# A gap in the scratch of the query and key parts: loads in runs of 2 KB, stores per batch

## The reference

```python
# layer 0: one head over all 1024 features, causal; ffn: 8 experts (shared weights + LoRA), top 2
# layer 1: attention of 16 heads, each the difference of two softmaxes over halves of 8 features
Q, K, V = (proj(Wq), proj(Wk), proj(Wv))                  # (b, 16, n, 16)
Q1, Q2 = jnp.split(Q, 2, axis=-1); K1, K2 = jnp.split(K, 2, axis=-1)
A1 = where(causal, Q1 @ K1.T * scaling, -inf); A2 = where(causal, Q2 @ K2.T * scaling, -inf)
attn = softmax(A1) - lam * softmax(A2)
O = attn @ V; O = O / rms(O) * rms_scale * (1 - LAMBDA_INIT); s = O @ Wo.T
# layer 1 ffn: 32 experts of 64 inner features (gate, up, down), top 8 by sigmoid, and a shared one
```

## Time and profile before

| | |
|---|---|
| median of 3 runs | 596.47 us (593.23 to 597.14) |
| the profiled execution, own time | 595.78 us |
| its span in the trace | 593.8 us |
| PE busy | 495.8 us (83%) |
| DVE, ACT, POOL busy | 393.3, 288.0, 266.4 us |
| mean granted TensorE clock | 0.934 of full |
| moved by DMA | 46.02 MB in 30,842 packets |

### The profile page before, as it was taken

How to read it: one execution, slowest core, us unless ns; L and a number is a source line. 1 busy time by engine, 2 the same in 40 slices (tenths; PEclk the granted TensorE clock), 3 DMA queues, 4 the chain that set the end, 5 groups by cost and what they waited for, 6 DMA issues and landing times.

```text
span 593.8 us, 8610 instructions
## 1 busy us (share of the span) xinstructions
PE 495.8 (83%) x3104; PEld 238.9 (40%) x3104; DVE 393.3 (66%) x796; ACT 288.0 (48%) x460; POOL 266.4 (45%) x223
## 2 busy tenths in 40 slices
PE   4865883988996999989947998999984991999995
PEld 4532631443443454443514453444431450444442
DVE  2426612879986786689844894669892971785674
ACT  1432450056775344576642445447660571447742
POOL 6122230134766406446431367326653364327973
PEclk9996796999999899999986999899996996899999
DMA  8502442212241311113330132013430142112111
GB/s 295 199 1 63 118 123 81 81 57 55 74 124 57 98 71 54 54 54 107 100 104 19 36 85 86 11 54 90 137 104 31 41 104 71 43 35 75 37 35 37
DMA packets 30842, 46.02 MB, mean 78 GB/s; under 512 B 4464, under 2 KB 18896, under 8 KB 28624
## 3 DMA queue, kind: packets, MB, share of 16 engines
q1 hardware_dynamic: 30800, 45.47, 25.4%
HBM read 37.47 MB, written 7.60 MB: 76 GB/s over the span
## 4 chain that ended last, share of the span: by engine, by line
PE 42%; DMA 24%; DVE 12%; SPq 10%; ACT 4%; issue 4%; POOL 3%; POOLq 1%; DVEq 0%; ACTq 0%
DMA ka<-parts_scratch 23%; SPq L515 8%; PE bank L728 6%; PE bank L737 5%; PE bank L749 5%; PE scores L769 4%; PE scores L763 4%; DVE nmax L1271 3%; PE scores L679 2%; PE bank L824 2%; PE scores L702 2%; PE bank L850 1%; DVE tmp L1124 1%; POOL gb L1070 1%; PE bank L837 1%
## 5 line engine op out<-in xcount | busy, mean ns | idle before, releaser
L1271 DVE TENSOR_REDUCE nmax<-scores 128x4 f32<-128x1024 f32 (+1 forms) x96 | 113.9, 1218 | 82.7 <-PE scores L769 82.3
L1070 POOL TENSOR_TENSOR gb<-gb,wb 128x512 f32<-128x512 f32 x64 | 84.1, 1314 | 155.6 <-ACT gb L978 145.2
L1063 POOL TENSOR_SCALAR_AFFINE_SELECT pk<-pk 128x512 f32<-128x512 f32 (+1 forms) x96 | 82.9, 872 | 80.4 <-ACT pk L991 79.7
L991 ACT ACTIVATE pk<-scores 128x1024 f32<-128x1024 f32 x96 | 95.6, 1024 | 40.2 <-PE scores L769 40.0
L975 ACT ACTIVATE gt<-bank,bgh 128x512 f32<-128x512 f32 (+1 forms) x68 | 46.8, 688 | 90.4 <-PE bank L728 81.5
L763 PE MATMUL scores<-mask_h,ident_h 64*128 64x256 bf16 (+2 forms) x384 | 40.1, 288 | 57.2 <-DMA ka<-parts_scratch 53.8
L728 PE MATMUL bank<-xnt,wg 128*128 128x512 f32 x128 | 72.1, 646 | 0.0
L749 PE MATMUL bank<-h,wd 128*128 128x512 f32 x128 | 69.6, 638 | 0.0
L737 PE MATMUL bank<-xnt,wu 128*128 128x512 f32 x128 | 68.5, 617 | 0.8 <-DVE h L1250 0.7
L1243 DVE SCALAR_TENSOR_TENSOR h<-gt,gb 128x512 f32<-128x512 f32 x64 | 50.3, 786 | 17.3 <-POOL gb L1070 12.5
L1250 DVE SCALAR_TENSOR_TENSOR h<-bank,bu,h 128x512 f32<-128x512 f32 x64 | 48.1, 751 | 16.4 <-PE bank L737 14.5
(11 more groups left out here) (191 smaller groups left out, 738.3 us busy)
## 6 DMA issues: line engine op xcount, KB each, us to landing
wb<-wt_scratch SPq DMA_DIRECT2D x64, 256.0 KB, 4.1
parts_scratch<-parts SPq DMA_DIRECT2D x48, 128.0 KB, 2.0
qa<-parts_scratch SPq DMA_DIRECT2D x16, 192.0 KB
ka<-parts_scratch SPq DMA_DIRECT2D x16, 192.0 KB
qa<-parts_scratch SPq DMA_DIRECT2D x16, 128.0 KB
ka<-parts_scratch SPq DMA_DIRECT2D x16, 128.0 KB
x<-in_x SPq DMA_DIRECT2D x4, 256.0 KB, 2.6
ha<-in_wkq SPq DMA_DIRECT2D x1, 1024.0 KB, 4.9
```

The costliest lines, as they stand in the source:

```text
L991: A(dst.rearrange("p (h m) q -> p m h q", m=2), pairs[pair_of(step)][:, :, :].rearrange("p m (h q) -> p m h q", q=cols), ACT.Exp, scale=SC ...
L1063: pool.affine_select(out=dst, in_=dst, compare_op=ALU.is_ge, fill=0.0, base=0, pattern=[[0, heads], [1, P]], channel_multiplier=-1).then_i ...
L1070: pw(gb[:, c % 2, :], gb[:, c % 2, :], wb[:, k % 2, j % 2, :], ALU.mult).then_inc(s_ga_done, 1)
L1271: V.tensor_reduce(dst, src, AX, ALU.max, negate=True).then_inc(s_nmax_done, 1)
```

## The change

The scratch gets a gap behind every fourth head: its last two dimensions (16 heads, 256 tokens) become (4 groups, 4 + 1 heads, 256 tokens), of which the fifth head is never written or read. A row of 16 heads is then four runs of 1,024 elements (2 KB), 2.5 KB apart. The loads of `fetch` name four runs for each row; their number (12 in a fetch), their rows and their bytes stay. The stores no longer fit one access pattern for both batches, so each is issued once for each batch: 24 of 64 KB in a chunk in place of 12 of 128 KB, still in runs of 512 bytes. The waits count the larger number of stores.

```diff
-                   qk_ps=4, qk_rest=4, part1=4, part2=4, part3=4, parts_stored=16 * 12, v_ps=2, v_sb=2,
+                   qk_ps=4, qk_rest=4, part1=4, part2=4, part3=4, parts_stored=16 * 24, v_ps=2, v_sb=2,
...
                                     sp.wait_ge(done, at(c, name, 2 * n + f + 1))
-                                    dst = t["parts_dram"][c, n, :, r, f * DH:(f + 1) * DH, :, :]
-                                    sp.dma_start(dst.rearrange("b d h t -> (d h) b t"),
-                                                 parts[:, a, 2 * n + f, :].rearrange("p (b t) -> p b t", b=CB)).then_inc(s_parts_stored, 16)
+                                    for b in range(CB):
+                                        dst = t["parts_dram"][c, n, b, r, f * DH:(f + 1) * DH, :, 0:GH, :]
+                                        sp.dma_start(dst.rearrange("d g h t -> (d g) h t"),
+                                                     parts[:, a, 2 * n + f, b * SEQ:(b + 1) * SEQ]).then_inc(s_parts_stored, 16)
...
-                                    src = t["parts_dram"][c, n, b, first:first + width, m * DH:(m + 1) * DH, :, :]
+                                    src = t["parts_dram"][c, n, b, first:first + width, m * DH:(m + 1) * DH, :, 0:GH, :]
                                     sp.dma_start(dst[row:row + width * DH, b, :, :], src).then_inc(s_qk_in[b], 16)
...
-    t["parts_dram"] = nc.dram_tensor("parts_scratch", (CHUNKS, 2, CB, 3, 2 * DH, HEADS, SEQ), BF16, kind="Internal").ap()
+    t["parts_dram"] = nc.dram_tensor("parts_scratch", (CHUNKS, 2, CB, 3, 2 * DH, GROUPS, GH + 1, SEQ), BF16, kind="Internal").ap()
```

More of the change, by code:

```diff
@@ L498, in steps @@
                                     sp.wait_ge(done, at(c, name, 2 * n + f + 1))
-                                    dst = t["parts_dram"][c, n, :, r, f * DH:(f + 1) * DH, :, :]
-                                    sp.dma_start(dst.rearrange("b d h t -> (d h) b t"),
-                                                 parts[:, a, 2 * n + f, :].rearrange("p (b t) -> p b t", b=CB)).then_inc(s_parts_stored, 16)
+                                    for b in range(CB):
+                                        dst = t["parts_dram"][c, n, b, r, f * DH:(f + 1) * DH, :, 0:GH, :]
+                                        sp.dma_start(dst.rearrange("d g h t -> (d g) h t"),
+                                                     parts[:, a, 2 * n + f, b * SEQ:(b + 1) * SEQ]).then_inc(s_parts_stored, 16)
                     elif kind == "fetch":
                         b = rest[0]
-                        sp.wait_ge(s_parts_stored, at(c, "parts_stored", 16 * 12))
+                        sp.wait_ge(s_parts_stored, at(c, "parts_stored", 16 * 24))
                         if c:
@@ L932, in front @@
                     if c and name == "queries1":
-                        act.wait_ge(s_parts_stored, at(c - 1, "parts_stored", 16 * 12))
+                        act.wait_ge(s_parts_stored, at(c - 1, "parts_stored", 16 * 24))
                     first = 0 if name == "queries1" else 2
```

## The result

The changed kernel takes **623.67 us** (median of 4 runs, 623.05 to 625.26) against 596.81 for the kernel before: ratio 1.0468, interval 1.0422 to 1.0513. It is slower by 26.9 us; the forecast was 611.0 with a range of 599 to 622. The direction was right and the size too small, and the time lies outside the range. The profiled execution takes 625.26 us, its span is 623.2 us.

The account below looks back on a forecast made before the run. Bound by `ka` fetches that two of sixteen engines carry while PE waits. Loads 9.1 + PE's clock 0.9 + stores 4.7 and 0.5 = 15.2 us on the profiled 595.78 gives 611.0 us, range 599 to 622.

Parts of the forecast that it names:

- What bounds the kernel: Fetches of `ka`: seven on the chain, each bound by two engines holding 68 rows; PE idles 53.8 us for them.
- The loads: Four 2 KB packets in place of one 8 KB: 1.3 us more a fetch, +9.1 us over seven fetches.
- the `x` window: Load of `x` alone, 48.0 to 49.6 us: 2 KB in 87 ns, +13% a row, 2.65 us a fetch.
- The stores: 12 more for each chunk on SP at 0.46 us, 24 in 11.0 us: chunk 1 +4.7, chunk 3 +0.5.
- The cover: Gaps and following waits on SP hide the extra stores: chunks 0 and 2 cost nothing, chunk 3 +0.5 us.
- SP held in a fetch: If the queue counts packets, SP is held amid each fetch; costed at nothing, as later work uses the same engines.
- rival 3: SP stuck within fetches, `wb` loads behind four of them start late: +10, so 621 us; chance 0.25 together with rival 4.
- Rival 4: Load packets cost what the `x` row gives or more: 18.6 for 9.1, 620.5 us; chance 0.25 together with rival 3.
- PE's clock: Longer fetch 1/1 makes PE idle, so one pair of matmuls runs at the 1.2 GHz level: +0.9 us (0 to 2).
- Rival 2: The gap spreads the reads, so fetches end faster: 581 us, or 590 with 9.1 for packets; chance 0.11.

Follow-up runs that it names:

- The order by half: Kernel before with the scratch reordered so a load's rows follow with one pitch, no gap, 12 stores in a chunk: 537.74 us, ratio 0.900.
- with 12 stores: Changed kernel storing batch 0 alone, 12 stores of 64 KB in a chunk, both batches loading batch 0's parts: 606.69 us, ratio 1.0187.
- plain stores: Kernel before with 24 stores in a chunk, one for each batch, no gap, loads unchanged: 603.71 us, ratio 1.014.

## Why the prediction was wrong, point by point

1. **What bounds the kernel: right.** Fetches that two engines carry and PE waits for. With the same bytes spread over more engines, 50 of the 53.8 us of PE's waits went. The order by half was chosen by the Trainium skill's rule on the number of engines (DMA: Bandwidth & Descriptors, "Why a DMA increments its semaphore by 16 and not by 1"), and the trace agrees that more engines then work: the share reaches 1.00, and the count of small packets fits 36 engines for three loads in place of 13.
2. **The loads: right in kind, smaller than forecast.** Predicted +9.1 over seven fetches, measured +6.1, and +6.6 with 12 stores. The tail of a fetch in the changed kernel has PE idle and two engines at 51 GB/s where it was 53:

```profile
203.00:209.00 6.00, 0.00 (x0) 0.00 (x0) 0.00 (x0) 0.00 (x0) 0.00 (x0) 0.50 0.13 51
```

   That is 4% and not the 6% I took, let alone the 13% of the `x` window, much of which may be its start, as I had noted. Tails of other fetches differ by 2% only (51 and 50, 49 and 48 GB/s in windows of 5 us), so this rate is known to a few per cent; the sum of the fetches, +6.1 against 1.0 with unchanged loads, is the firmer number. The Trainium skill's 3 cycles a packet (DMA: Bandwidth & Descriptors, "Why small descriptors are slow (HBM only)") made it 5.1 us, nearer than my sum. For 512 bytes the same rule gives 16 x 19 cycles against 259, an estimate of 17% of 7 x 21.0, 25.5 us; 37.8 were measured, so it is too mild there, if nothing but the packets made these fetches longer.
3. **The stores: this is the step that failed.** "Half the bytes in each issue take that away, so I take 0.46" gave 24 stores 11.0 us. They take 15.5 to 15.8 in chunks 0, 2 and 3, 0.645 to 0.66 from issue to issue, and 16.7 in chunk 1. I had priced them from eight DMAs of 16 partitions and from the old stores, whose two sides have equal shapes; the row in the order of instructions, 32x4x256 against 128 partitions, was in front of me, and I read no price for an unequal shape off it, though the kernel before had one: loads with 24 rows against 3 x 8 cost SP 0.70 us, the plain ones of 8 rows 0.43. With plain stores at 0.43 the step comes out nearly as forecast, +7.1 against 5.2, though 24 of them still take 12.0 to 12.5 us and not 11.0.
4. **The cover: right for the assumed price, gone with the real one.** Chunks 0, 2 and 3 had 12.4, 11.8 and 11.4 us for the stores. 11.0 fit, 15.5 do not; each lost 3.6 to 4.2 us where I had 0, 0 and 0.5, and chunk 1 lost 10.2 for 4.7. In chunks 2 and 3 the sum had no term for the maxima's rows behind the stores, for which PE now waits 3.4 and 3.0 us. Of the 16.8 us that the sum lacks in the stores, 11.3 are here and 5.5 in chunk 1. I kept an upper end of 0.53 us for the price, which gives some 9 us of stores by the same covers and not 22.0. The range reached 622 only through rivals 3 and 4, whose causes did not come, so that it ends so near the measured time is luck.
5. **SP held in a fetch: seen, and nearly free,** as costed. SP needs 15.4 to 17.4 us for a fetch's issues and not 7.7, and what stands behind the fetches is not later for it: from the landing of fetch 0/0 to the next store 61.1 us pass against 62.2, behind 2/0 28.6 against 28.8, behind 3/1 87.7 against 89.0. Only behind 2/1 it is 42.4 against 40.9, with PE at a colder clock (next point). So rival 3, with its 621 us the nearest number, had the hold right and its price wrong. That the fetch itself is no longer for the hold is likely, since its sum grew by 6.1 us only, but no run has the packets without the hold. Rival 4 wanted 18.6 us for the packets; 6.1 rule it out.
6. **PE's clock: +0.9 did not come where I put it.** After fetch 1/1 the granted clock stayed at 1.00, the level of 2.4 GHz, though PE had waited 1.9 us for that fetch and not 0.6:

```profile
245.80:252.00 6.20, 6.04 (x38) 2.95 (x39) 5.25 (x6) 0.57 (x1) 5.80 (x2) 1.00 0.28 95
```

   A colder clock came after fetch 2/1 instead. The same three microseconds, from 3 us behind its landing, before and after:

```profile
374.57:377.57 3.00, 3.00 (x7) 1.31 (x6) 0.85 (x2) 1.15 (x2) 0.00 (x0) 0.76 0.00 1
```

```profile
399.09:402.09 3.00, 3.00 (x5) 1.35 (x4) 1.38 (x2) 0.12 (x1) 0.00 (x0) 0.50 0.01 3
```

   PE had waited 4.3 us for that fetch and not 3.3. The stretch from its landing to chunk 3's first store is 1.5 us longer (42.4 for 40.9, mean clock 0.92 for 0.96), inside the 0 to 2 that I had given for the clock, at another fetch; it lies in "all the rest" of the table.

7. **Rival 2, a gap that spreads the reads:** nothing of it. With gaps behind every eighth, fourth or each head no fetch on the chain was shorter by more than 0.8 us, and their sum grew each time, with the gap behind every eighth head by no more than unchanged loads do.

Sum by the runs: 22.0 (stores) + 6.1 (loads) = 28.1 against 15.2 forecast; the profiled executions differ by 29.5, of which 3.0 are start-up, and the medians by 26.9. PE's wait for `ka` came to 66.2 us, close to the 68 I had named, but that is luck: the loads gave less and chunk 1's stores more, where this wait went from 4.8 to 16.2 us.

## What to carry to other kernels

A DMA has a price on the queue that issues it, apart from its bytes, and it depends on how its two sides are cut: take it from a DMA of the same shape on both sides as yours, and multiply it by the count before calling it hidden, since a cover of 11.8 us hides 11.0 and not 15.5. When a transfer bounds a kernel, divide its rate by the rate of one engine first: here two of sixteen carried it, and reordering the scratch so that a load's rows have one pitch was worth 10%, while cutting its runs from 8 to 2 KB cost 1% (to 512 bytes, 7%). When a queue fills, time from last issue to landing shrinks without anything getting faster; measure from the first issue.

## What the runs showed of the hardware that was not expected

- SP's time for a DMA from the same queue: 0.29 to 0.35 us for loads of 8 to 24 rows, whole on both sides, one after the other, 0.43 for plain stores of 128 runs back to back, 0.60 for stores of 128 against 32 x 4 or 16 x 8, 0.63 to 0.70 for loads of 16 or 24 rows against 2 or 3 x 8. A gap did not change the price where it left both sides cut alike (0.43 for one-batch stores with and without it). Where it cut one side's rows into four runs, loads of one pitch went from 0.31 to 0.57 and more. A plain load of 8 rows cost 0.43 between loads of the dear kind and 0.31 among plain ones, so its own shape is not all; the neighbours may count.
- SP is held the longer the more packets there are: from the last issue to the landing 20.8 us with packets of 8 KB, 14.5 with 2 KB, 8.6 with 512 bytes, in the same fetch 3/1.
- Packets of 4 KB and 8 KB were equal within 0.1 us a fetch in the mean of seven (single fetches differ by -0.7 to +1.6 us); 2 KB cost 0.9 us a fetch, 512 bytes 5.4 us, on two engines that hold 68 rows of 8 KB each.
- Sixteen engines busy on loads of 8 to 24 partitions moved 176 GB/s together, 11.0 each, and in the tail, at a share of seven, 75 GB/s; two moved 53, 26.5 each.
